# Four turns in the body of ScalarE's loop: a three-layer attention network with a cross-attention head

## The reference

```python
def attention(q, k, v, src_mask, dam, zero_pad, gammas):
    scores = jnp.einsum('bhqd,bhkd->bhqk', q, k) / math.sqrt(dk)
    sc = jax.nn.softmax(jnp.where(damb, scores, NEG), axis=-1)
    ...
    dist = jnp.sqrt(jnp.clip((disttot - distcum) * pos[None, None], 0.0, None))
    te = jnp.clip(jnp.exp(dist * gamma), 1e-05, 100000.0)
    scores = jax.nn.softmax(jnp.where(damb, scores * te, NEG), axis=-1)
    return jnp.einsum('bhqk,bhkd->bhqd', scores, v)

y = transformer_layer(1, qa, qa, qa, True, P(0))     # with a feed-forward part
x = transformer_layer(1, q, q, q, False, P(1))       # without
x = transformer_layer(0, x, x, y, True, P(2))        # with; values come from y
```

## Time and profile before

| | |
|---|---|
| median of 3 runs | 3373.2 us (3372.44 to 3375.31) |
| profiled execution | 3372.7 us, of it the span of the trace 3371.0 us |
| busy share of the span | PE 89%, DVE 83%, ACT 81%, PEld 65%, POOL 23% |
| the chain of work that ended last | PE 55%, DVE 19%, issue 12%, SP's queue 4%, ACT 3% |
| TensorE's granted clock, mean | 0.97 |

### The profile page before, as it was taken

The page is one execution under the profiler, slowest core; times in us unless marked ns, Lnnn a source line. Parts: engine busy times, 40 slices in busy tenths (PEclk is TensorE's granted clock), DMA queues, the critical chain, the costliest instruction groups (busy, mean ns, idle before and its releaser), DMA issues.

```text
span 3371.0 us, 71476 instructions
## 1 busy us (share of the span) xinstructions
PE 2990.0 (89%) x19520; PEld 2204.6 (65%) x19520; DVE 2802.8 (83%) x5825; ACT 2715.9 (81%) x10244; POOL 775.8 (23%) x1111
## 2 busy tenths in 40 slices
PE   2689999999999999999999999999999998999986
PEld 1466676666676666676666666666666666666664
DVE  3688988888988888988888988888988888988883
ACT  1688888888888888888888888888888887888883
POOL 1212222222222222222222221222221222221221
PEclk9799999999999999999999999999999999999998
DMA  5000101000101000101100001000101101001100
GB/s 160 20 25 25 32 25 33 27 26 25 30 25 33 27 26 25 30 25 33 28 26 25 29 24 33 29 26 25 28 24 33 29 28 29 24 24 33 29 17 10
DMA packets 166407, 101.66 MB, mean 30 GB/s; under 512 B 36697, under 2 KB 165709, under 8 KB 166221
## 3 DMA queue, kind: packets, MB, share of 16 engines
q1 hardware_dynamic: 166220, 99.97, 10.4%
HBM read 56.26 MB, written 10.01 MB: 20 GB/s over the span
## 4 chain that ended last, share of the span: by engine, by line
PE 55%; DVE 19%; issue 12%; SPq 4%; ACT 3%; DMA 2%; POOL 1%; DVEq 0%; ACTq 0%; POOLq 0%
PE gen_ps L623 17%; PE gen_ps L755 13%; PE gen_ps L709 6%; PE gen_ps L673 4%; SPq L556 4%; PE gen_ps L690 3%; DVE E L920 3%; PE scores_ps L664 2%; ACT X L802 2%; PE scores_ps L652 2%; DVE X L929 2%; PE gen_ps L718 2%; PE gen_ps L631 2%; PE gen_ps L684 2%; DVE res L964 2%
## 5 line engine op out<-in xcount | busy, mean ns | idle before, releaser
L802 ACT ACTIVATE X<-X,nm 128x128 f32<-128x128 f32 x1536 | 596.0, 405 | 56.7 <-DVE nm L945 55.8
L802 ACT ACTIVATE E<-scores_ps,nm 128x128 f32<-128x128 f32 x1536 | 542.3, 406 | 24.2 <-DVE nm L912 24.0
L912 DVE TENSOR_REDUCE nm<-scores_ps 128x8 f32<-128x1024 f32 x320 | 390.3, 1220 | 182.0 <-PE scores_ps L652 113.6
L623 PE MATMUL gen_ps<-f_buf,up_w 128*128 128x256 f32 x2048 | 466.1, 383 | 0.8 <-ACT f_buf L459 0.8
L1052 POOL TENSOR_SCALAR_AFFINE_SELECT X<-X 128x1024 f32<-128x1024 f32 x192 | 211.2, 1100 | 1100.8 <-DVE X L939 1100.0
L755 PE MATMUL gen_ps<-down_w,hidden 128*128 128x256 f32 x2048 | 459.7, 379 | 0.0
L802 ACT ACTIVATE X<-scores_ps,nm 128x128 f32<-128x128 f32 x1024 | 362.3, 400 | 116.6 <-issue 60.9
L673 PE MATMUL gen_ps<-ident,X 128*128 128x128 f32 x2560 | 380.0, 283 | 79.2 <-ACT xv_t L476 39.8
L929 DVE SCALAR_TENSOR_TENSOR X<-E,rz,decay 128x128 f32<-128x128 f32 x1536 | 431.0, 350 | 3.7 <-DVE E L920 0.5
L920 DVE TENSOR_TENSOR_SCAN E<-chain,E 128x1024 f32<-128x1024 bf16 x192 | 429.8, 2238 | 0.0
L623 PEld LDWEIGHTS gen_ps<-f_buf,up_w 128*128 128x128 f32 x2048 | 382.7, 191 | 70.5 <-issue 21.9
(11 more groups left out here) (124 smaller groups left out, 5491.7 us busy)
## 6 DMA issues: line engine op xcount, KB each, us to landing
k_diag<-k_f SPq DMA_DIRECT2D x768, 32.0 KB, 1.9
xk_diag<-xk_f SPq DMA_DIRECT2D x1024, 8.0 KB, 1.8
ctx_f<-in_ctxT SPq DMA_DIRECT2D x32, 256.0 KB, 3.2
ctx_t<-in_ctx SPq DMA_DIRECT2D x32, 256.0 KB, 2.8
x_f<-in_xT SPq DMA_DIRECT2D x32, 256.0 KB, 2.6
x_t<-in_x SPq DMA_DIRECT2D x32, 256.0 KB, 2.6
cx_f<-in_ctxT SPq DMA_DIRECT2D x32, 256.0 KB, 2.7
out<-out_t SPq DMA_DIRECT2D x32, 256.0 KB, 2.2
```

Of the source, the lines that this page charges most:

```text
L623: mm = nc.tensor.matmul(ps[:, i * T:(i + 1) * T], w[:, k, c * P:(c + 1) * P], src[:, k, :], start=(k == 0), stop=(k == C - 1))
L802: a = nc.scalar.activation(dst[:, cols], src[:, cols], ACT.Exp, bias=minus_max[:, h:h + 1], accum_out=sums[:, h:h + 1])
L912: nc.vector.tensor_reduce(nm1[:, UNIT[u], :], unit_heads(scores_ps[SLOT[u]][:, :]), AX_X, ALU.max, negate=True).then_inc(max1_done, 1)
```

## The change

`run_turns` takes a parameter `body`, the turns in one body of the loop, 1 for PE, DVE, POOL and SP, and 4 for ACT. With 4, `first` is 32 - 29 // 4 * 4 = 4: ACT runs turns 0 to 3 straight, then 7 passes over a body of four turns, then turns 32 and 33 straight. With 1, `first` is 3 as before. The semaphore counts of the second to fourth turn of a body come from `it + 1` to `it + 3`. No list, wait or count differs.

```diff
-BEFORE = range(LATEST + 1)
-LOOP = (LATEST + 1, GROUPS)
 AFTER = range(GROUPS, GROUPS + LATEST)

-def run_turns(eng, turn_of):
-    for it in BEFORE:
+def run_turns(eng, turn_of, body=1):
+
+    first = GROUPS - (GROUPS - LATEST - 1) // body * body
+    for it in range(first):
         turn_of(Now(it))
-    with eng.Fori(*LOOP) as it:
-        turn_of(Now(it))
+    with eng.Fori(first, GROUPS, body) as it:
+        for i in range(body):
+            turn_of(Now(it + i if i else it))
     for it in AFTER:
         turn_of(Now(it))
@@ in ACT's program
-            run_turns(act, turn_of)
+            run_turns(act, turn_of, 4)
```

## The result

The changed kernel takes 3339.4 us (median; 3338.7 to 3341.2) where the kernel before, run beside it, takes 3374.3: a ratio of 0.990 with an interval of 0.988 to 0.991. The gain is 34.9 us by these medians and 33.1 us by the two profiled spans (3371.0 and 3337.9); the forecast was 31.2 us and 3342.0. Lines of `kernel.py` stand one further down in the changed kernel: L803 is the L802 of the earlier trace rows.

A forecast was written before the change was run, and what follows sets the result against it. The prediction took a dependence loop through several engines, including ACT's branch back, as the bound; 22 branches removed at 1.42 us save 31.2 us, added instructions and clock 0, so 3373.2 becomes 3342.0 us, range 3331 to 3357.

The forecast's parts named there:

- The gain per branch: At ACT's branch back: each of 22 removed saves PE's mean wait for `xv_t`, 1.42 us, in all 31.2 us.
- the cover of 0.76 us: At ACT's branch back: PE's own transposes and matmuls cover 0.75 us of ACT's 2.17 us idle.
- The working that moved ACT forward: At a turn change without branch: ACT, moved by its 2.31 us idle, is 0.8 us early and PE waits for nothing.
- nothing beyond PE's own wait can be had: At the turn change: the `x_tok` path, without ACT, sets the time next, so a branch gains 1.42 us, not 2.17.
- The low end: From the loop's entry, PE's `a_tok` transposes to `k` matmuls: 1.18 us gain per branch, 26.0 us in all.
- The six remaining branches: ACT's branches over the longer body: the same 2.17 us idle each; with the longest idle, six would cost 2.6 us more.
- The added waits and register operations: In ACT's longer body: more waits and operations, fewer fused groups, net -4 to +8 us, taken as 0.
- Fetched too late: Rival, ACT's longer body: packets away from the branch hold ACT up too, slower at 3501 us; chance 4%.
- The whole idle comes back: Rival, at ACT's branches: the full 2.17 us each is gained, 47.8 us, giving 3325.4 us; chance 5%.
- No gain: Rival, at turn changes: PE's time is waited away later or the idle belongs to every turn, 3373 us; chance 8%.
- The clock: Over the loop's unequal turns: no change from the granted clock, with 8 us allowed either way.

The follow-up runs named there:

- the holds: Increments of an otherwise unused semaphore on ACT at the 21 turn changes that lost their branch, against the changed kernel: 3367.6 us with 32, 3340.4 us with 16.
- a hold of 0.67 us: 16 increments of an unused semaphore on ACT at each of the 21 turn changes without a branch, against the changed kernel: 3340.4 us.
- The long holds: 32 increments of an unused semaphore on ACT at each of the 21 turn changes without a branch, against the changed kernel: 3367.6 us.

## Why the prediction was right

**The gain per branch.** It took PE's wait, 1.42 us, and not ACT's idle, 2.17 us. The six branches that stay cost PE 1.47 us each, two turns in a body gave 1.50 us a branch, and the holds show the cover of 0.76 us directly. The working that moved ACT forward and found it 0.8 us early was right as well: a hold of 0.67 us is free, and ACT now waits for PE at `h_buf`. What was wrong in it is the sentence that nothing beyond PE's own wait can be had: with all turns unrolled 1.84 us a branch came, and the rest stands under the clock below. The low end, 1.18 us from the entry into the loop, was too low, by about the 0.35 us of a delay that only the entry has.

**What was set at nothing.** The six remaining branches keep their idle of 2.2 us over a body of 1011 instructions as built: the price does not grow with the way back. The added waits and register operations leave no idle by issue inside the body. PE's waits for `x_tok` went from 115.0 to 115.2 us.

**The rivals.** *Fetched too late*: the packets do arrive in straight code, 3 in a turn without a branch where 5 had come, but none of them holds ACT up, and with all turns unrolled none does in the loop. Its premise, that the packets are ACT's, was right; that those away from a branch delay it was not. *The whole idle comes back*: the waits of PE and the holds exclude it as a mechanism, though all turns unrolled came out beyond it per branch (51.5 / 28 = 1.84 us), for another reason. *No gain* is excluded by the two kinds of turn change. The Trainium skill, Runtime: NRT & Kernel Launch, section Instruction fetch mechanics, says that a taken branch to code that is not held waits for a fetch, and the traces agree, with 2.6 us on ACT and 2.8 us on DVE. Its room of 512 instructions for most engines is not the length of a loop that stays loaded here, since 383 were fetched again on every pass of ACT.

**The clock.** It was taken at 0 with 8 us either way, and the rest of the gain fits this term. One pass of four turns should take 4 x 100.97 - 3 x 1.42 = 399.6 us; from 825.52 to 1224.80, the starts behind two of ACT's idles, it took 399.3. The turns in it are not alike. Stretches of the changed kernel from PE's start on `x_tok`, the one behind the turn with the branch first (us, busy time by engine, PEclk, DMA, GB/s):

```profile
907.97:1007.80 99.83, 92.98 (x610) 69.02 (x611) 86.94 (x181) 84.90 (x322) 23.97 (x34) 0.97 0.10 28
1007.80:1107.01 99.21, 92.35 (x610) 68.22 (x610) 86.93 (x181) 84.90 (x322) 23.97 (x34) 0.98 0.10 28
...
1206.25:1307.23 100.98, 92.58 (x611) 68.23 (x611) 87.03 (x181) 84.79 (x322) 23.98 (x35) 0.98 0.10 28
...
907.97:914.80 6.83, 6.83 (x25) 5.58 (x26) 4.91 (x14) 4.19 (x20) 1.72 (x3) 0.61 0.18 59
1007.80:1014.60 6.80, 6.79 (x29) 5.27 (x30) 5.27 (x15) 4.23 (x21) 1.72 (x3) 0.75 0.17 55
```

The same with all turns unrolled:

```profile
1305.87:1404.85 98.98, 92.14 (x610) 68.23 (x610) 86.93 (x181) 84.78 (x322) 23.97 (x34) 0.98 0.10 28
...
1305.87:1312.70 6.83, 6.83 (x31) 5.55 (x32) 5.52 (x15) 4.37 (x21) 1.72 (x3) 0.75 0.24 57
```

In each turn PE stands still for 3.4 us ahead of `x_tok`, and behind this idle part of the time runs at the lower of the two clocks, 1.2 in place of 2.4 GHz. In the turn that follows the branch this part is longer (granted clock of the first 6.8 us: 0.61) than in the next one (0.75). PE's busy time for the same 610 instructions is 0.63 us more there, and the turn is 0.62 us longer. The turn that holds the branch is 1.8 us longer than one without, of which PE's wait is 1.5; the prediction had 1.4. With all turns unrolled the turn shown has the 0.75 and takes 99.0 us, and so do its neighbours.

That is where the 11.7 us on top lie: of the 100.97 us of a turn before, 1.42 us were PE's wait, and 0.56 us more went with it. PE's busy time gave up 12.9 us of the run, 0.46 us for each of 28 branches, with the same instructions. That the lower clock is the cause of all of it is not shown: turns of 99.2 and 99.0 us with the same 0.75 differ in busy time as well (92.35 and 92.14 us), and nothing was run that moves the clock alone. The long holds show the same in the other direction: with a wait of 0.99 us in each, turns of 100.08 and 101.16 us stand beside each other, the longer with the lower clock and with 1.07 us more of PE's busy time.

```profile
1414.57:1515.73 101.16, 93.31 (x611) 69.08 (x611) 87.05 (x181) 84.81 (x322) 23.97 (x35) 0.97 0.10 28
1515.73:1615.81 100.08, 92.24 (x611) 68.28 (x611) 87.01 (x181) 84.68 (x322) 23.97 (x34) 0.98 0.10 28
```

So the forecast of 3342.0 was 2.6 us too high. PE's waits for `xv_t` fell by 31.0 us (39.8 to 8.8), as forecast, and PE's busy time by 3.1 us more (2990.0 to 2986.9), which was set at nothing. In the version without branches this second term was worth some 12 us, more than the range of 8 us either way gave it.

## What to carry to other kernels

Look for an idle "by issue" that stands once per loop turn with instruction packets beside it, and price it by what the waiting engine downstream waits, not by the idle itself: of 2.17 us here 1.42 counted on ACT, and of 2.8 us behind DVE's branch nothing. If a pass is just above what stays loaded, shortening it (319 instructions in place of 383 on ACT) removes the idle as surely as unrolling does, and without making code longer; else unroll that engine's loop alone, as far as it goes. Where neither can be done, put the branch at a place where the engine waits anyway or still has work queued. The first was worth 28.9 us on ACT; both together hid the whole fetch on DVE.

## What was not expected of the hardware

- Behind a branch back into loaded code the next instruction comes 0.2 to 0.3 us later (ACT with 255 and 319 instructions in a pass, DVE with 284). Into code that has to be fetched again it takes 2.4 to 3.0 us on ACT in the kernel before and 2.8 to 3.1 us on DVE. In the kernel with the moved branch one piece of issue is 3.0 us, at a place where a load of 256 KB runs; that the load is the cause was not tried.
- ACT fetched a loop of 383 instructions again on every pass, and 319 not. DVE fetched 559 again, and 284 not.
- A branch is issued ahead of the end of the work before it: on DVE by 1.9 us, on ACT by 0.5 us. This part of the fetch is free.
- Straight code of 29 turns ran on ACT without one idle by issue in the loop, with 2 packets between 1310 and 1410 us.
- Turns that are all alike came with a gain beyond the waits that went: 98.99 us in place of 100.97 us, with 1.42 us of waits gone.
